# 16-column attention: where the softmax division is made

## The chip, the cores and the metric

The kernel runs on one core of one Trainium2 chip. The metric is the device time of one execution in microseconds. The kernel before was timed three times: 897.86, 899.01 and 900.95 us, median 899.01 us.

The core has five engines that matter here, each with its own in-order instruction stream, which meet through semaphores: TensorE (PE, with its weight loads PEld), VectorE (DVE), ScalarE (ACT), GpSimd (POOL) and SyncE (SP), which only issues DMAs. GpSimd does not touch the matmul accumulators (PSUM, 8 banks); TensorE writes them, VectorE and ScalarE read them.

## The reference

64 images of 96x96x3 are cut into 36 patches each (2304 tokens of 192 features). The tokens then go through: an embedding, a causal attention with 12 heads of 64 columns ("wide", the code calls the stage attn1), a layer with attention and an MLP, and a second layer with attention and a mixture of experts. The attentions of the last two layers are the ones that change. Each has 12 heads of 16 columns over the 36 tokens of one image:

```python
# attention of the MLP layer (stage attn2)
a = softmax(einsum('bhnd,bhmd->bhnm', q, k) * hd ** -0.5, axis=-1)     # hd = 16
o = einsum('bhnm,bhmd->bhnd', a, v).transpose(0, 2, 1, 3).reshape(B, N, C)
o = o @ w_proj + b_proj
# attention of the expert layer (stage attn3): the same with a bias -slope[h] * |n - m| on the scores
```

softmax is exp(s - max) divided by its sum over m. The division commutes with the product by v: it may be done to the probabilities, or to o.

## The kernel before, in words

Both attentions are made by one function, `narrow_stage` (L808). It works on units of two images (72 tokens, `UNIT`), 32 units in all, in groups of four units (288 tokens, `WIDE`), 8 groups. Every engine walks steps k = 0 .. 34 in program order; step k holds pieces of several units, so that the stage is a software pipeline. Within a step, in order:

- TensorE (`tensor`): `scores(k)`, six matmuls with q as weights and head-masked keys as data (L1032, L1036), into PSUM banks 2 and 3 or 4 and 5 in turn; `mix(k-3)`, eight matmuls of 108 rows by 36 columns, probabilities times values (L1064), into bank 6; the next group's work, by k mod 4: transposes of x (L983), projections of q and k (L994 to L998, two of three chunks, then one), values (L1013); `turn(k-2)`, four transposes of the probabilities (L1047), into bank 6 as well, so that it waits for `copy_z(k-3)`; then `project_out(t)` (L1073, L1074) for each tile of 128 tokens that is complete, 18 tiles in all.
- VectorE (`vector`): `take_scores(k)`: row maximum and subtraction (attn2: L1302, L1304), or bias addition and row maximum (attn3: L1295, L1300); `sum_up(k-1)`: row sums of the exponentials, 100x432 to 100x12 (L1311), and the reciprocal of these 12 columns (L1316); by k mod 4 the split of x (L1262, L1263), the masked keys (L1270, L1271) and in attn2 the layer norm in front (L1237 to L1253); `post_norm` in attn3 (L1335), and `add_residual(t)` (L1320, in attn3 also L1325 to L1329).
- ScalarE (`scalar`): `exponentiate(k-1)` (L1176), `copy_z(k-3)` from bank 6 into the ring z_t (L1193, L1195), the group's roundings and copies, `copy_turned(k-2)` (L1183).
- GpSimd (`gpsimd`): in attn3 `shift(k)`, subtraction of the maximum (L938); `normalise(k-1)`, the 100x432 probabilities times the broadcast reciprocal (L931); small powers (L920, L925), and the split of weights for the stage that follows (L2599 to L2619).
- SyncE (`sync`): once a group, after its last value block is copied, `spread_values` issues nine DMAs (L897) that place the values block by block; `mix` of the group's first unit waits for them. Weight loads for later stages follow in the same queue.

The values carry a column of ones (L951), which brings the bias row of the output projection in. While attn2 ends, the MLP begins (`tail`); attn3 is followed by the experts. `keep_going` (L337) issues matmuls without a use where TensorE would stand still.

## Time and profile before

| | us |
|---|---|
| median of three runs | 899.01 |
| profiled execution | 903.05 |
| its span | 901.3 |
| TensorE busy | 818.9 |
| VectorE busy | 542.0 |
| ScalarE busy | 439.9 |
| GpSimd busy | 408.7 |

The span is what the profile covers; 1.75 us of the profiled execution lie around it. attn2 takes the stretch from about 292 to 412 us, attn3 that from about 534 to 677 us. "Busy" counts each instruction from its start to its end. The ends of matmuls are modelled, so a busy TensorE can still have room.

### The profile page before, as it was taken

To read this page: it belongs to the slowest core of one execution; us is meant where nothing else is said; L and a number is where in the kernel's file an instruction comes from. 1 tells how busy PE (TensorE), PEld (TensorE's weight loads), DVE (VectorE), ACT (ScalarE), POOL (GpSimd) and SP (SyncE) were. 2 spreads that over 40 slices of the span, in tenths; PEclk is the share of its full clock that TensorE was granted. 3 is DMA by queue.
4 is the path that set the end of the run, shared out by engine and by line. 5 is a ranking of instruction groups with operands and counts; after the bars stand their busy time and mean duration, and the time that the engine had idled before them with its cause. 6 is when DMAs were issued, how large, how long until landed. Compare 5 with 4: busy or idle time off the path is not lost. (4 is left out here: it accounts for less than half of the span.)

```text
span 901.3 us, 21350 instructions
## 1 busy us (share of the span) xinstructions
PE 818.9 (91%) x7767; PEld 733.5 (81%) x7767; DVE 542.0 (60%) x1467; ACT 439.9 (49%) x1094; POOL 408.7 (45%) x489
## 2 busy tenths in 40 slices
PE   9899999999998898987999989888879999999973
PEld 8889998899997676766999976666657899899973
DVE  2235565556665898993763337788966622467645
ACT  0246555555644576763345527566626221355523
POOL 1534444344444544342442236767841455244444
PEclk9999999999999999996999989898979999999996
DMA  9910111111110232225200013623200111333252
GB/s 308 265 51 21 31 27 37 31 32 30 37 37 2 35 67 26 34 22 172 24 1 1 1 27 50 157 47 65 46 3 2 36 60 63 81 99 107 77 170 94
DMA packets 103942, 55.78 MB, mean 62 GB/s; under 512 B 67264, under 2 KB 94512, under 8 KB 103840
## 3 DMA queue, kind: packets, MB, share of 16 engines
q1 hardware_dynamic: 99248, 45.99, 21.2%
q0 software_dynamic: 3792, 7.84, 2.5%
q8 instruction: 64, 1.05, 0.5%
q10 hardware_dynamic: 800, 0.59, 0.2%
q14 instruction: 38, 0.31, 0.1%
HBM read 29.81 MB, written 13.97 MB: 49 GB/s over the span
## 5 line engine op out<-in xcount | busy, mean ns | idle before, releaser
L931 POOL TENSOR_TENSOR attn_prob<-attn_prob,attn_recip 100x432 f32<-100x432 f32 x64 | 58.6, 916 | 67.1 <-DVE attn_recip L1316 66.6
L450 POOL TENSOR_TENSOR attn_prob_x<-attn_prob,attn_recip 100x864 f32<-100x864 f32 x32 | 52.6, 1644 | 52.8 <-DVE attn_recip L759 52.8
L1892 POOL DMA_INDIRECT results<-moe_hid_shared x43 | 41.1, 955 | 58.1 <-ACT moe_hid_shared L2107 58.1
L1602 ACT ACTIVATE mlp_hid<-psum,columns 128x384 f32<-128x384 f32 x72 | 38.1, 580 | 41.4 <-PE psum L96 41.4
L1047 PE MATMUL psum<-ident,attn_prob 100*108 100x100 f32 x256 | 35.5, 264 | 21.4 <-POOL attn_prob L931 12.9
L1047 PEld LDWEIGHTS psum<-ident,attn_prob 100*108 100x108 f32 x256 | 26.1, 138 | 27.2 <-POOL attn_prob L931 18.7
L1064 PEld LDWEIGHTS psum<-attn_prob_t,attn_values 108*49 108x49 f32 (+1 forms) x1024 | 33.7, 132 | 15.5 <-ACT attn_prob_t L1183 6.7
L1176 ACT ACTIVATE attn_prob<-attn_prob 100x432 f32<-100x432 f32 x64 | 36.1, 564 | 19.0 <-POOL attn_prob L938 17.8
L2082 ACT ACTIVATE moe_silu<-psum 128x384 f32<-128x384 f32 x36 | 17.7, 491 | 56.5 <-PE psum L107 56.5
L1064 PE MATMUL psum<-attn_prob_t,attn_values 108*49 108x36 f32 (+1 forms) x1024 | 36.0, 217 | 8.3 <-DMA attn_values<-attn_v_tok 5.0
L1555 PE MATMUL psum<-mlp_w_dn_s,mlp_hid 128*128 128x192 f32 (+2 forms) x306 | 42.6, 290 | 0.0
L436 POOL TENSOR_TENSOR attn_rstd<-attn_var_eps,neg_half 128x1 f32<-128x1 f32 x18 | 10.2, 568 | 71.3 <-DVE attn_var_eps L771 71.3
L1970 PE MATMUL psum<-w_dn_shared,moe_hid_shared 128*128 128x192 f32 x216 | 38.7, 342 | 3.7 <-DVE moe_hid_shared L2257 3.7
L1555 PEld LDWEIGHTS psum<-mlp_w_dn_s,mlp_hid 128*128 128x128 f32 x306 | 42.0, 191 | 0.0
L1970 PEld LDWEIGHTS psum<-w_dn_shared,moe_hid_shared 128*128 128x128 f32 x216 | 37.8, 201 | 4.1 <-DVE moe_hid_shared L2257 4.0
L686 ACT ACTIVATE attn_z_t<-psum 128x432 f32<-128x432 f32 (+2 forms) x32 | 16.2, 507 | 50.6 <-PE psum L566 50.5
L938 POOL TENSOR_TENSOR attn_prob<-attn_prob,attn_row_max 100x432 f32<-100x432 f32 x32 | 29.1, 910 | 25.7 <-DVE attn_row_max L1300 25.7
L2496 PE MATMUL psum<-embed_w_tok,embed_patches 128*128 128x192 f32 x216 | 37.1, 329 | 3.9 <-DMA embed_patches<-in_x 3.1
L2496 PEld LDWEIGHTS psum<-embed_w_tok,embed_patches 128*128 128x128 f32 x216 | 34.8, 190 | 5.9 <-DMA embed_patches<-in_x 4.6
L576 PE MATMUL psum<-w_o,attn_z_t 128*128 128x192 f32 x216 | 38.7, 329 | 0.9 <-ACT attn_z_t L686 0.6
L1455 POOL TENSOR_TENSOR mlp_rstd<-mlp_var_eps,neg_half 128x1 f32<-128x1 f32 x18 | 10.6, 587 | 63.3 <-DVE mlp_var_eps L1671 63.3
L1311 DVE TENSOR_REDUCE attn_row_sum<-attn_prob 100x12 f32<-100x432 f32 x64 | 38.0, 594 | 2.0 <-ACT attn_prob L1176 1.7
(474 smaller groups left out, 2790.5 us busy)
## 6 DMA issues: line engine op xcount, KB each, us to landing
embed_patches<-in_x SPq DMA_DIRECT2D x8, 768.0 KB, 14.5
sorted_rows<-mlp_pad_zeros SPq DMA_DIRECT2D x1, 4214.0 KB, 15.6
moe_hid_shared<-sorted_rows SPq DMA_DIRECT2D x43, 98.0 KB, 2.1
attn_v<-attn_v_tok SPq DMA_DIRECT2D x16, 216.0 KB
attn_values<-attn_v_tok SPq DMA_DIRECT2D x96, 27.0 KB
side_raw_a<-in_w_gu_dram SPq DMA_DIRECT2D x8, 288.0 KB, 3.2
side_raw_b<-in_w_gu_dram SPq DMA_DIRECT2D x16, 144.0 KB, 3.4
h_rows<-results SPq DMA_DIRECT2D x6, 288.0 KB, 5.4
```

The lines of the kernel that those rows point to most:

```text
L450: nc.gpsimd.tensor_tensor(prob_x[k % 2][:, :, :, :], prob[k % 3][:, :, :].rearrange("p h (a n) -> p h a n", a=1) .to_broadcast([QP, HEADS, ...
L576: last = nc.tensor.matmul(out_ps, z_t[:, c, at:at + P], w_o[:, c, :], start=(c == 0), stop=(c == chunks - 1))
L931: nc.gpsimd.tensor_tensor(pr, pr, recip[k % 2][:, :].rearrange("p (h a) -> p h a", a=1) .to_broadcast([QP, HEADS, SEQ]), ALU.mult).then_in ...
L1047: last = nc.tensor.transpose(bank(6)[0:3 * SEQ, n * P:n * P + QP], flat[:, n * 3 * SEQ:(n + 1) * 3 * SEQ], ident[0:QP, 0:QP])
L1064: last = nc.tensor.matmul(ps[r:r + m, n // 2, a * SEQ:(a + 1) * SEQ], v[:, n, 0:m], prob_t[k % 2][:, n, a, :], start=True, stop=True)
L1176: nc.scalar.activation(prob[k % 3][:, :, :], prob[k % 3][:, :, :], ACT.Exp).then_inc(S["exp_done"], 1)
L1311: nc.vector.tensor_reduce(row_sum[:, :], prob[k % 3][:, :, :], axis=AX.X, op=ALU.add).then_inc(S["sum_ready"], 1)
L1555: last = nc.tensor.matmul(bank(3 + t)[:, 0:w.shape[1]], hid_step(n)[:, t * MT:(t + 1) * MT], w, start=(n == 0), stop=(n == 17), skip_group ...
L1602: nc.scalar.activation(hid_step(n), bank(n % 3)[:, 0:MW], ACT.Gelu, bias=b_up[:, c:c + 1]).then_inc(S["gelu_done"], 1)
L1892: nc.gpsimd.indirect_dma_start(out=results, out_offset=bass.IndirectOffsetOnAxis(ap=x_in[j % x_ring][:, D:D + 1].bitcast(U32), axis=0), in ...
L1970: last = nc.tensor.matmul(bank(4 + n % 2)[:, 0:D], hid_of(i)[:, c, t * P:(t + 1) * P], w_dn_shared[:, c, :], start=(c == 0), stop=(c == sh ...
L2496: last = nc.tensor.matmul(out_bank(t), patches[:, t, c, :], w_tok[:, c, :], start=(c == 0), stop=(c == chunks - 1))
```

## The change

Nothing is divided before the mixing any more. The exponentials go to `turn`, `copy_turned` and `mix` as they are, each a step (turn) or a step less a piece (mix) earlier than before. A new piece `add_up(k)` multiplies the turned probabilities by a constant block `head_ones` (108x64: ones where row and column belong to the same head of the three), which puts each head's sum, over 36 rows, into the 16 columns of that head, in the same layout as z: 128 x 2 x 72. The block is made once, by a memset and three affine_select of GpSimd, each waiting for the one before. VectorE inverts this whole block out of bank 5 (`invert_sums`), ScalarE copies z unchanged into `z_raw`, and GpSimd multiplies both into z_t (`divide_z`). `sum_up` and `normalise` are gone. The scores have one pair of banks instead of two, the probabilities two buffers instead of three, and the turned probabilities have bank 4 for themselves.

```diff
-    prob = [sb(f"prob{p}", [QP, HEADS, SEQ]) for p in range(3)]
+    prob = [sb(f"prob{p}", [QP, HEADS, SEQ]) for p in range(2)]
-    row_sum = sb("row_sum", [QP, HEADS])
-    recip = [sb(f"recip{p}", [QP, HEADS]) for p in range(2)]
+    head_ones = sb("head_ones", [3 * SEQ, 64])
+    recip = [sb(f"recip{p}", [P, 2, UNIT]) for p in range(2)]
+    z_raw = [sb(f"z_raw{p}", [P, 2, UNIT]) for p in range(2)]
...
+    scores_ps = psum[:, 2 * BANK:4 * BANK].rearrange("p (s n) -> p s n", s=4)[:, 0:3, 0:4 * SEQ].rearrange(
+        "p s (h n) -> p s h n", h=4)
+    turned_ps = bank(4).rearrange("p (g a n) -> p g a n", g=4, a=2)
     z_ps = bank(6)[:, 0:2 * UNIT].rearrange("p (c n) -> p c n", c=2)
+    sums_ps = bank(5)[:, 0:2 * UNIT].rearrange("p (c n) -> p c n", c=2)
...
 # gpsimd
-        def normalise(k):
+        def divide_z(k):
             pool.wait_ge(S["recip_ready"], k + 1)
+            pool.wait_ge(S["z_copied"], k + 1)
...
+            ins = nc.gpsimd.tensor_tensor(z_t[:, :, at:at + n], z_raw[k % 2][:, :, 0:n], recip[k % 2][:, :, 0:n],
+                                          ALU.mult)
+            if n < UNIT:
+                ins = nc.gpsimd.tensor_tensor(z_t[:, :, 0:UNIT - n], z_raw[k % 2][:, :, n:UNIT],
+                                              recip[k % 2][:, :, n:UNIT], ALU.mult)
+            ins.then_inc(S["z_divided"], 1)
...
         clear(0)
+        nc.gpsimd.memset(head_ones[:, :], 1.0).then_inc(S["ones_placed"], 1)
+        pool.wait_ge(S["ones_placed"], 1)
+        nc.gpsimd.affine_select(out=head_ones[:, 0:48], in_=head_ones[:, 0:48], compare_op=ALU.is_ge, fill=0.0, base=0,
+                                pattern=[[-SEQ, 3], [0, 16]], channel_multiplier=1).then_inc(S["ones_placed"], 1)
...
         clear(1)
...
+            if k >= 3:
+                divide_z(k - 3)
             if bias_hk is not None and k < units:
                 shift(k)
-            if 1 <= k <= units:
-                normalise(k - 1)
...
 # tensor, scores(k)
-            if k >= 2:
-                pe.wait_ge(S["scores_taken" if bias_hk is not None else "shifted"], k - 1)
+            if k >= 1:
+                pe.wait_ge(S["scores_taken" if bias_hk is not None else "shifted"], k)
 # turn(k)
-            pe.wait_ge(S["normalised"], k + 1)
+            pe.wait_ge(S["exp_done"], k + 1)
             if k >= 1:
                 pe.wait_ge(S["turned_copied"], k)
-                pe.wait_ge(S["z_copied"], k)
...
+        def add_up(k):
+            pe.wait_ge(S["turned_copied"], k + 1)
+            if k == 0:
+                pe.wait_ge(S["ones_placed"], 4)
+            else:
+                pe.wait_ge(S["recip_ready"], k)
+            for n in range(4):
+                r, m = 64 * (n % 2), 64 if k == 0 else 49
+                last = nc.tensor.matmul(sums_ps[r:r + m, n // 2, :], head_ones[:, 0:m],
+                                        prob_t[k % 2][:, n, :, :].rearrange("p a q -> p (a q)"), start=True, stop=True)
+            last.then_inc(S["added_up"], 1)
 # project_out(t)
-            pe.wait_ge(S["z_copied"], -(-P * (t + 1) // UNIT))
+            pe.wait_ge(S["z_divided"], -(-P * (t + 1) // UNIT))
 # order of a step
-            if k >= 3:
-                mix(k - 3)
...
             if 2 <= k < units + 2:
-                turn(k - 2)
+                add_up(k - 2)
+                mix(k - 2)
+            if 1 <= k <= units:
+                turn(k - 1)
...
 # scalar: copy_turned(k - 1) instead of (k - 2), at the same place; copy_z(k)
-            ins = nc.scalar.activation(z_t[:, :, at:at + n], z_ps[:, :, 0:n], ACT.Copy)
+            if k >= 2:
+                act.wait_ge(S["z_divided"], k - 1)
+            nc.scalar.activation(z_raw[k % 2][:, :, :], z_ps[:, :, :], ACT.Copy).then_inc(S["z_copied"], 1)
 # vector, take_scores(k)
-            if k >= 3:
-                dve.wait_ge(S["turned"], k - 2)
+            if k >= 2:
+                dve.wait_ge(S["turned"], k - 1)
...
-        def sum_up(k):
-            dve.wait_ge(S["exp_done"], k + 1)
-            dve.wait_ge(S["recip_ready"], k)
-            nc.vector.tensor_reduce(row_sum[:, :], prob[k % 3][:, :, :], axis=AX.X, op=ALU.add
-                                    ).then_inc(S["sum_ready"], 1)
-            dve.wait_ge(S["sum_ready"], k + 1)
+        def invert_sums(k):
+            dve.wait_ge(S["added_up"], k + 1)
             if k >= 2:
-                dve.wait_ge(S["normalised"], k - 1)
-            nc.vector.reciprocal(recip[k % 2][:, :], row_sum[:, :]).then_inc(S["recip_ready"], 1)
+                dve.wait_ge(S["z_divided"], k - 1)
+            nc.vector.reciprocal(recip[k % 2][:, :, :], sums_ps[:, :, :]).then_inc(S["recip_ready"], 1)
...
+            if k >= 3:
+                invert_sums(k - 3)
             if k < units:
                 take_scores(k)
-            if 1 <= k <= units:
-                sum_up(k - 1)
```

## Rows read from the trace of the kernel before

**Rows 1.** The page's busy times: engine, busy us, share of the span, instructions.
```profile
PE 818.9 (91%) x7767; PEld 733.5 (81%) x7767; DVE 542.0 (60%) x1467; ACT 439.9 (49%) x1094; POOL 408.7 (45%) x489
```

**Rows 2.** Busy time by stretch: steady parts of attn2 and attn3.
```profile
core 0: us, PE busy (x) PEld busy (x) DVE busy (x) ACT busy (x) POOL busy (x), PEclk, DMA share, GB/s
309.00:396.00 87.00, 79.91 (x1067) 64.19 (x1068) 78.18 (x174) 64.24 (x177) 37.06 (x54) 0.98 0.24 37
552.00:650.00 98.00, 85.84 (x1093) 67.86 (x1094) 83.45 (x189) 62.88 (x161) 73.66 (x84) 0.93 0.39 79
```

**Rows 3.** Groups of VectorE by shape: xcount, busy us, mean ns, idle before.
```profile
L1311 DVE TENSOR_REDUCE attn_row_sum<-attn_prob 100x12 f32<-100x432 f32 x64 | 38.0, 594 | 2.0 <-ACT attn_prob L1176 1.7
L1302 DVE TENSOR_REDUCE attn_row_max<-psum 100x12 f32<-100x432 f32 x32 | 19.1, 596 | 2.0 <-PE psum L1036 1.6
L1316 DVE RECIPROCAL attn_recip<-attn_row_sum 100x12 f32<-100x12 f32 x64 | 14.6, 228 | 2.2
L1325 DVE BATCH_NORM_STATS2 attn_stats<-h_rows 128x6 f32<-128x192 f32 x18 | 6.5, 361 | 0.6
L1320 DVE TENSOR_TENSOR x_tok<-psum,h_rows 128x192 f32<-128x192 f32 x18 | 6.2, 347 | 16.4 <-PE psum L1074 16.2
```

**Rows 4.** The same view, small and 144-column operations of VectorE.
```profile
L1329 DVE TENSOR_SCALAR attn_var_eps<-attn_mean_var 128x1 f32<-128x1 f32 x18 | 2.8, 154 | 0.6
L2199 DVE TENSOR_TENSOR moe_earlier<-psum,moe_iota 128x144 f32<-128x144 f32 x1 | 0.3, 308 | 0.2 <-PE psum L1948 0.2
L2752 DVE TENSOR_SCALAR columns<-columns 64x1 f32<-64x1 f32 x1 | 0.1, 132 | 0.0
```

**Rows 5.** Timeline (start us, us) of TensorE in attn2: mix, half a projection, turn.
```profile
313.05 0.53 PE L1064 MATMUL psum<-attn_prob_t,attn_values 108*49 108x36 f32 x16
...
315.08 0.52 PE L1073 MATMUL psum<-w_o,attn_z_t 128*128 128x192 f32 x2
...
318.79 0.51 PE L1047 MATMUL psum<-ident,attn_prob 100*108 100x100 f32 x4
```

**Rows 6.** Waits, 300 to 412 us (attn2): us in total, times, longest.
```profile
POOL attn_prob L931 <- DVE attn_recip L1316: 63.6, 28, 6.1
PE psum L1047 <- POOL attn_prob L931: 3.7, 5, 1.4
PE psum L1047 <- ACT attn_z_t L1193: 3.7, 3, 2.3
```

**Rows 7.** Waits, 545 to 672 us (attn3).
```profile
PE psum L1047 <- POOL attn_prob L931: 9.2, 6, 3.2
DVE h_rows L1320 <- PE psum L1074: 10.0, 4, 5.6
PE psum L1047 <- ACT attn_z_t L1193: 3.4, 8, 0.9
```

**Rows 8.** Groups of GpSimd by shape.
```profile
L931 POOL TENSOR_TENSOR attn_prob<-attn_prob,attn_recip 100x432 f32<-100x432 f32 x64 | 58.6, 916 | 67.1 <-DVE attn_recip L1316 66.6
L461 POOL TENSOR_TENSOR h_rows<-h_rows,vectors 128x192 f32<-128x192 f32 x18 | 10.3, 596 | 10.1 <-DVE vectors L2775 10.1
L2604 POOL TENSOR_TENSOR w_router_a_lo<-side_raw_a,w_router_a_hi 128x10 fp32r<-128x10 f32 x1 | 0.2, 208 | 0.0
```

**Rows 9.** One line of VectorE, L1335: duration min, median, max.
```profile
L1335 DVE TENSOR_SCALAR h_rows<-h_rows,attn_mean_var,attn_rstd x18: 379/419/3193, 560.6 to 676.8; 128x192 f32<-128x192 f32 x18
```

**Rows 10.** Timeline around the values' DMAs and the first mixes in attn3.
```profile
542.34 7.51 SPq L897 DMA_DIRECT2D attn_values<-attn_v_tok  x9
551.16 0.66 PE L1064 MATMUL psum<-attn_prob_t,attn_values 108*64 108x36 f32 x16 [1.49 <-DMA attn_values<-attn_v_tok]
...
581.18 0.89 PE L1064 MATMUL psum<-attn_prob_t,attn_values 108*49 108x36 f32 x16 [3.48 <-DMA attn_values<-attn_v_tok]
```

**Rows 11.** Timeline: one projection matmul in each attention's head.
```profile
293.09 0.29 PE L995 MATMUL psum<-ring_a_lo,w_qkv_a_hi 128*128 128x288 f32 x1
...
535.72 0.44 PE L995 MATMUL psum<-ring_a_lo,w_qkv_a_hi 128*128 128x288 f32 x1
```

More of the change, by code:

```diff
@@ L953, in gpsimd @@
         clear(0)
+        nc.gpsimd.memset(head_ones[:, :], 1.0).then_inc(S["ones_placed"], 1)
+        pool.wait_ge(S["ones_placed"], 1)
+        nc.gpsimd.affine_select(out=head_ones[:, 0:48], in_=head_ones[:, 0:48], compare_op=ALU.is_ge, fill=0.0, base=0,
+                                pattern=[[-SEQ, 3], [0, 16]], channel_multiplier=1).then_inc(S["ones_placed"], 1)
+        pool.wait_ge(S["ones_placed"], 2)
+        nc.gpsimd.affine_select(out=head_ones[:, 0:48], in_=head_ones[:, 0:48], compare_op=ALU.is_ge, fill=0.0,
+                                base=SEQ - 1, pattern=[[SEQ, 3], [0, 16]], channel_multiplier=-1
+                                ).then_inc(S["ones_placed"], 1)
+        pool.wait_ge(S["ones_placed"], 3)
+        nc.gpsimd.affine_select(out=head_ones[:, 48:64], in_=head_ones[:, 48:64], compare_op=ALU.is_ge, fill=0.0,
+                                base=SEQ - 1, pattern=[[0, 16]], channel_multiplier=-1
+                                ).then_inc(S["ones_placed"], 1)
         clear(1)
@@ L1040, in turn @@
         def turn(k):
[L1041 removed]
+            pe.wait_ge(S["exp_done"], k + 1)
             if k >= 1:
                 pe.wait_ge(S["turned_copied"], k)
[L1044 to L1045 removed]
+            flat = prob[k % 2][:, :, :].rearrange("p h n -> p (h n)")
             for n in range(4):
[L1047 removed]
+                last = nc.tensor.transpose(bank(4)[0:3 * SEQ, n * P:n * P + QP],
                                            flat[:, n * 3 * SEQ:(n + 1) * 3 * SEQ], ident[0:QP, 0:QP])
@@ L1221, in scalar @@
                 side.round_step(act, g - 1)
-            if 2 <= k < units + 2:
-                copy_turned(k - 2)
+            if 1 <= k <= units:
+                copy_turned(k - 1)
             if g < groups and j == 1:
```

33 lines of the change are left out of this document (10 added, 23 removed).

## The prediction

> **What bounds the kernel now.** I read the busy times first: TensorE is busy 91% of the span, VectorE 60% [rows 1]. That is an average over stages. By stretch the two attentions look otherwise: in attn2's steady part TensorE has 79.91 of 87 us and VectorE 78.18, in attn3's 85.84 and 83.45 of 98 [rows 2]. So two engines are within 2% of each other, and ends of matmuls are modelled while VectorE's are not. Which of them sets the pace I take from who waits. In attn2 GpSimd waits 63.6 us for the reciprocal, that is for VectorE to come to it, while VectorE sat idle only 2.0 us before all its row maxima and 2.0 us before all its row sums [rows 3, 6]: VectorE works through its queue with 8.8 of 87 us idle, and the reader should see in it the engine to which time must not be added. TensorE's own waits are for what comes through the long chain exponential, sum, reciprocal, product, turn: 3.7 us for GpSimd and 3.7 us for the copy of z in attn2, 9.2 and 3.4 us in attn3 [rows 6, 7]. In attn3 VectorE waits 10.0 us for the output projection, 5.6 us of it at once [rows 7], behind a mix that stood 3.48 us for the values' DMAs [rows 10]. The other stages are not touched.
>
> **VectorE, the term that decides.** Removed per unit: the row sum, 594 ns, and the reciprocal of 12 columns, 228 ns [rows 3], 0.82 us. Added: one reciprocal of 144 columns. No row shows it at that size. From the rows: an operation has a part that does not grow. VectorE rows of one column take 132 and 154 ns, one of 144 columns 308 [rows 4], so the rate of ordinary operations is (308 - 154) / 143 = 1.08 ns a column. The reciprocal of 12 columns takes 228. With 132 ns fixed, 96 ns are left for 12 columns, 8.0 ns each, and 144 columns take 132 + 144 x 8.0 = 1.28 us. With 154 ns fixed it is 6.2 ns each and 1.04 us. From below: if the excess were a fixed cost of the operation, 132 further columns at the ordinary rate give 228 + 143 = 0.37 us [rows 4]. From above: with nothing fixed, 228 x 12 = 2.74 us. I take 1.28: a fixed part must exist, the one-column rows measure it, and 228 ns lies far off the 166 ns (154 + 11 x 1.08) that a 12-column operation of ordinary rate would take. The change is then 1.28 - 0.82 = +0.46 us a unit, 32 x 0.46 = +14.7 us in each attention if VectorE sets the pace throughout.
>
> **TensorE.** Added per unit: four matmuls of 108x49 weights on 72 columns. A mix is eight of 36 columns with the same weights' size, the same 288 columns in all, and takes 0.53 us [rows 5]; so I take 0.5 us, and bound it by half of that and by 0.6. Over 64 units 32 to 34 us. Removed is no matmul, only waits before the turn, for GpSimd and for the copy of z: 7.4 us in attn2 and 12.6 us in attn3 [rows 6, 7]. Against VectorE: in the steady part of attn2 (87 us, 25 units of 3.5 us) VectorE needs 78.2 + 25 x 0.46 = 89.7 us of work and TensorE 79.9 + 12.5 = 92.4, of which the modelled ends are a part; with the 8.8 us that VectorE now loses between instructions and in short waits, 98.5 us. VectorE stays the later one, and the addition on TensorE is hidden behind it. If it is not hidden it is the first rival below.
>
> **GpSimd.** 916 ns a unit go (L931). A product of 128x144 lies between 10 columns, 208 ns, and 192, 596 ns [rows 8]: 208 + 134 x 2.13 = 0.49 us; two of 16 units wrap in the ring and pay a second start. GpSimd gets 64 x 0.42 = 27 us back, off the path. But L1335 on VectorE, 0.379 us at its shortest, stretches to 3.193 us when GpSimd runs beside it, 18 of them with a median of 0.419 [rows 9]; with GpSimd less busy I give back 2 us in attn3 (bounds 0 and 5).
>
> **Order and buffers.** `invert_sums(k-3)` stands first in VectorE's step. `add_up(k-2)` waits for it, and behind it on TensorE stand mix, turn and the output projection. `add_residual`, the last piece of VectorE's step, waits for that projection. So in a step with a complete tile (18 of 32) the loop is: reciprocal 1.28, add_up 0.5, mix 0.53, turn 0.51, projection 0.8 (two of 0.4), residual 0.35 [rows 3, 5], some 4.0 us; in attn3 its statistics follow, 0.36 and two operations under 0.2 with a wait each, 4.8 us. VectorE's own work in a step without group work is 1.28 + 1.2 (two like the 0.596 of L1302) + 0.35 = 2.8 us, in attn3 4.1 with the statistics and L1335. The gap of about 1 us counts only where k mod 4 brings no group work, five or so steps in a stage, and a part of it is in today's waits: +3 us in each (bounds 0 and 6). One pair of banks for the scores: scores(k) waits for take_scores(k-1), which VectorE does right after its reciprocal, before TensorE is through with step k-1; nothing. Two buffers of probabilities: take_scores(k) waits for turn(k-2), a step earlier on TensorE; nothing. In attn3 VectorE has 14.6 us of idle in 98 [rows 2]; the chain through sum, reciprocal and product no longer stands in front of the turn, so a part of that idle is work time now: -5 us (bounds 0 and -10).
>
> **The values' DMAs.** Nine issues take 7.51 us, and the first mix ran 8.8 us after the first of them, after a wait of 1.49 us [rows 10]. The mix of a group's first unit now stands at the end of the third step instead of the start of the fourth, in front of a turn and of the next scores. In steady state that leaves the rest of a step and two and a half more, of at least 3.5 us each, some 11 us, more than 8.8. At the head of each stage the wait is there, and scores(3) and a turn now stand behind it: +1 us each, +2. The stall of 3.48 us stays. Building head_ones, four short GpSimd instructions of some 0.2 us, as the one of 10 columns [rows 8], delays only the clearing of the second group's buffers and one small power behind it: +0.3.
>
> **Sum.** 14.7 + 14.7 (VectorE) + 6 (loop) - 5 (idle taken) - 2 (L1335) + 2 + 0.3 (heads of stages) = +30.7 us on the profiled execution's 903.05 us (span 901.3 and 1.75 around it): 933.8. The median of the runs is 4.0 us below the profiled one, so 929.7; I say 929.
>
> **The rivals.**
> - *TensorE sets the pace.* For: 92.4 us of work against 89.7 as computed above. Against: modelled ends, and VectorE's waits for it are short. Then the cost is 34 us less the 20 us of waits, +14: 913.
> - *The reciprocal is cheap, and the change pays.* The place is VectorE's queue; it decides from a 144-column reciprocal under the 0.82 us removed. At 0.37 us VectorE gives back 29 us. TensorE's 34 us then have to lie in its idle time, 7.1 of 87 and 12.2 of 98 us, which over both stages (scaled to 32 units each: 9 and 15 us) is 24, and in what a full clock would give back, 7% of some 120 us and 2% of another, 11 us: -1 at that, and -5 with L1335 as well: 894. Against it stands the 228 ns row.
> - *TensorE's clock.* It was granted 0.98 in attn2 and 0.93 in attn3 [rows 2]. A TensorE that waits for VectorE at each step stands still more often, and at the lower level (1.2 GHz) a projection matmul takes 0.44 us instead of 0.29 [rows 11], 0.15 more. A group has 15 of these and as many of the values, some 4 us in all with its other matmuls. If a third of its work fell there, +0.7 us in 16 groups, +11: 940.
> - *Nothing changes* because both engines had room: would need the loss of 0.46 us a unit to fall into VectorE's 9% idle, 8.8 us in 25 units against 11.5 added. It cannot be whole.
>
> **Chances.** Forecast 0.70, TensorE 0.12, clock 0.10, cheap reciprocal 0.06, nothing 0.02. The time is 929. A reciprocal of 1.04 us would take off 64 x 0.24 = 15 us (914), and the first rival lies at 913; no idle taken, no gain at L1335 and the loop at its upper bound add 13 (942). Range 910 to 944. A difference of 0.3% (2.7 us) is about what this kernel's measurement can tell. Faster 0.07, same 0.03, slower 0.90.
>
> **What would show it.** Right: a 144-column reciprocal of 1.2 to 1.35 us, x64; VectorE busy above 90% in both attentions; the group period 2 us longer in attn2, a little less in attn3; TensorE's waits now at add_up, for the reciprocal; GpSimd's product near 0.5 us; no wait for GpSimd before a turn. Wrong: a reciprocal under 0.8 us; VectorE idle rising while TensorE has none; granted clock under 0.9 in attn2.

## The result, and the profile after

| us | before | after |
|---|---|---|
| median, runs side by side | 899.96 (897.86 to 900.95) | 930.06 (927.59 to 934.26) |
| profiled execution | 903.05 | 927.59 |
| its span | 901.3 | 925.9 |

The ratio is 1.034, 95% interval 1.030 to 1.039. 929 was forecast, 910 to 944. The total came out; the reasons did so only in part.

First the busy times on the page, answering to [rows 1].

```profile
PE 846.4 (91%) x8279; PEld 745.8 (81%) x8279; DVE 548.8 (59%) x1403; ACT 436.1 (47%) x1086; POOL 385.7 (42%) x505
```

Then the two stretches of [rows 2].

```profile
309.00:396.00 87.00, 81.93 (x1165) 61.33 (x1162) 74.04 (x138) 55.99 (x158) 24.07 (x50) 1.00 0.23 36
552.00:650.00 98.00, 87.83 (x1118) 65.03 (x1117) 75.75 (x135) 57.25 (x140) 56.12 (x79) 0.93 0.37 75
```

The kernel is 25 us longer by its span, and VectorE's total busy time grew by 7. In both stretches its share fell: 78.18 to 74.04 of 87 us, 83.45 to 75.75 of 98. The second stretch exaggerates this, because attn3 begins 12.6 us later in the kernel after; over each kernel's own seven group periods (defined below) the share fell from 89% to 83% in attn2 and from 84% to 80% in attn3. An engine that sets the pace doesn't get idler when it is given more work.

The new operations on the page: xcount, busy us, mean ns of one, and what ended the idle time before.

```profile
L1340 DVE RECIPROCAL attn_recip<-psum 128x144 f32<-128x144 f32 x64 | 67.4, 1054 | 6.0 <-PE psum L1097 5.7
L938 POOL TENSOR_TENSOR attn_z_t<-attn_z_raw,attn_recip 128x144 f32<-128x144 f32 (+1 forms) x64 | 30.2, 472 | 114.6 <-DVE attn_recip L1340 78.2
L1097 PE MATMUL psum<-attn_prob_t,attn_head_ones 108*49 108x72 f32 (+1 forms) x512 | 31.1, 244 | 16.3 <-DVE attn_recip L1340 15.5
```

The reciprocal takes 1.054 us, not 1.28. The product takes 0.49 us whole (472 ns with the wrapped ones). TensorE has a new wait, 15.5 us for the reciprocal, in front of `add_up`.

Where the time is: SyncE's timeline (start us, duration) has the values' DMAs once a group, so that eight starts give seven periods of each stage. Before, the first and last of attn2 and the last of attn3 (attn3's first is the 542.34 of [rows 10]):

```profile
298.30 7.52 SPq L897 DMA_DIRECT2D attn_values<-attn_v_tok  x9
...
395.93 7.85 SPq L897 DMA_DIRECT2D attn_values<-attn_v_tok  x9
...
646.69 7.49 SPq L897 DMA_DIRECT2D attn_values<-attn_v_tok  x9
```

After, the first and last of both:

```profile
297.80 7.52 SPq L899 DMA_DIRECT2D attn_values<-attn_v_tok  x9
...
404.35 7.85 SPq L899 DMA_DIRECT2D attn_values<-attn_v_tok  x9
...
554.93 7.51 SPq L899 DMA_DIRECT2D attn_values<-attn_v_tok  x9
...
668.97 7.49 SPq L899 DMA_DIRECT2D attn_values<-attn_v_tok  x9
```

A group's period went from 97.63 / 7 = 13.95 us to 106.55 / 7 = 15.22 in attn2, and from 14.91 to 16.29 in attn3. By stretch, the 24.6 us of the span are: -0.5 up to attn2's first group, +8.9 over its seven periods, +4.2 from there to attn3's first (attn2's last group and attn3's start), +9.7 over attn3's periods, +2.3 behind them. All later runs are read by these two periods.

Who waits, 555 to 705 us of the kernel after, answering to [rows 7]:

```profile
DVE h_rows L1344 <- PE psum L1107: 19.3, 17, 3.6
PE psum L1097 <- DVE attn_recip L1340: 11.7, 10, 3.5
```

VectorE waits for the output projection, 19.3 us where it was 10.0 [rows 7] (12.2 over the whole of attn3 before), and TensorE waits for VectorE's reciprocal. Two engines that wait for each other are the sign of a loop. One step and the next, on both engines' timeline (weight loads, the scores, the projections, the values and other work left out):

```profile
627.25 0.36 DVE L1344 TENSOR_TENSOR h_rows<-psum,h_rows 128x192 f32<-128x192 f32 x1 [1.32 <-PE psum L1107]
...
629.60 0.46 PE L1097 MATMUL psum<-attn_prob_t,attn_head_ones 108*49 108x72 f32 x8 [0.78 <-DVE attn_recip L1340]
...
630.59 1.42 DVE L1299 SCALAR_TENSOR_TENSOR attn_keys_b<-psum,columns,head_mask 64x1152 f32<-64x1152 f32 x1
...
631.09 0.49 PE L1107 MATMUL psum<-w_o,attn_z_t 128*128 128x192 f32 x2
...
632.04 1.51 DVE L1359 TENSOR_SCALAR h_rows<-h_rows,attn_mean_var,attn_rstd 128x192 f32<-128x192 f32 x1
...
633.59 0.36 DVE L1344 TENSOR_TENSOR h_rows<-psum,h_rows 128x192 f32<-128x192 f32 x1
...
633.98 0.36 DVE L1349 BATCH_NORM_STATS2 attn_stats<-h_rows 128x6 f32<-128x192 f32 x1
...
634.74 1.06 DVE L1340 RECIPROCAL attn_recip<-psum 128x144 f32<-128x144 f32 x1
635.72 0.55 DVE L1323 TENSOR_TENSOR attn_prob<-psum,bias 100x432 f32<-100x432 f32 x1
...
635.95 0.61 PE L1097 MATMUL psum<-attn_prob_t,attn_head_ones 108*49 108x72 f32 x8 [1.78 <-DVE attn_recip L1340]
```

In the first of the two steps each engine waits for the other: VectorE 1.32 us for the projection, then TensorE 0.78 us for the reciprocal that stands behind the residual. In the second, VectorE waits for nothing: the projection of 631.09 was long done when VectorE came to its residual at 633.59. The sums that the second reciprocal inverts lay in the bank since about 630; it came at 634.74 because it is queued behind the masked keys, the post-norm, the residual and its statistics of the step before. TensorE stood 1.78 us for it, and its next `add_up` took 0.61 us instead of 0.46.

### The profile page after: what moved, and what is told of

It reads as the page before. It is cut to its first block and busy times, and to the rows that moved or that the text cites. A ratio compares the mean times of both kernels' runs of the same rounds, so it can differ in the third digit from the quotient of the medians.

```text
span 925.9 us, 22390 instructions
## 1 busy us (share of the span) xinstructions
PE 846.4 (91%) x8279; PEld 745.8 (81%) x8279; DVE 548.8 (59%) x1403; ACT 436.1 (47%) x1086; POOL 385.7 (42%) x505
## 5 line engine op out<-in xcount | busy, mean ns | idle before, releaser
L938 POOL TENSOR_TENSOR attn_z_t<-attn_z_raw,attn_recip 128x144 f32<-128x144 f32 (+1 forms) x64 | 30.2, 472 | 114.6 <-DVE attn_recip L1340 78.2
L1340 DVE RECIPROCAL attn_recip<-psum 128x144 f32<-128x144 f32 x64 | 67.4, 1054 | 6.0 <-PE psum L1097 5.7
L1217 ACT ACTIVATE attn_prob_t<-psum 108x288 f32<-108x288 f32 x64 | 26.2, 409 | 77.7 <-PE psum L1068 77.7
L1097 PE MATMUL psum<-attn_prob_t,attn_head_ones 108*49 108x72 f32 (+1 forms) x512 | 31.1, 244 | 16.3 <-DVE attn_recip L1340 15.5
L1097 PEld LDWEIGHTS psum<-attn_prob_t,attn_head_ones 108*49 108x49 f32 (+1 forms) x512 | 21.5, 131 | 29.2 <-issue 26.3
L1085 PE MATMUL psum<-attn_prob_t,attn_values 108*49 108x36 f32 (+1 forms) x1024 | 36.7, 217 | 6.1 <-ACT attn_z_raw L1224 4.0
L553 PE MATMUL psum<-ident,attn_prob_x 100*72 100x100 f32 x384 | 38.4, 249 | 0.0
L2281 DVE TENSOR_TENSOR moe_hid_shared<-psum,moe_silu 128x384 f32<-128x384 f32 x36 | 20.0, 556 | 30.8 <-PE psum L107 30.6
```

The costliest lines, as they stand in the source:

```text
L553: last = nc.tensor.transpose(bank(3 + p)[0:UNIT, n * P:n * P + QP], prob_x[k % 2][:, 4 * p + n, :, :].rearrange("p a n -> p (a n)"), ident ...
L938: ins = nc.gpsimd.tensor_tensor(z_t[:, :, at:at + n], z_raw[k % 2][:, :, 0:n], recip[k % 2][:, :, 0:n], ALU.mult)
L1085: last = nc.tensor.matmul(ps[r:r + m, n // 2, a * SEQ:(a + 1) * SEQ], v[:, n, 0:m], prob_t[k % 2][:, n, a, :], start=True, stop=True)
L1097: last = nc.tensor.matmul(sums_ps[r:r + m, n // 2, :], head_ones[:, 0:m], prob_t[k % 2][:, n, :, :].rearrange("p a q -> p (a q)"), start=T ...
L1340: nc.vector.reciprocal(recip[k % 2][:, :, :], sums_ps[:, :, :]).then_inc(S["recip_ready"], 1)
```

## The experiments

All were timed side by side with the kernel before, and the medians of before lie between 897.0 and 899.4 in these groups. "Period" is a group's, attn2 / attn3; before it is 13.95 / 14.91, after 15.22 / 16.29.

| kernel | us | ratio to before, 95% | period |
|---|---|---|---|
| after | 930.06 | 1.030 to 1.039 | 15.22 / 16.29 |
| after, copy in place of reciprocal | 914.61 | 1.012 to 1.022 | 15.07 / 15.13 |
| after, add_up twice | 933.31 | 1.033 to 1.047 | 15.83 / 17.01 |
| after, one sum matmul of four | 927.10 | 1.027 to 1.037 | 15.19 / 16.20 |
| after, two banks for sums | 939.97 | 1.042 to 1.052 | 16.04 / 17.18 |
| after, reciprocal ahead of residual | 911.48 | 1.008 to 1.017 | 15.37 / 15.89 |
| the same, mix early | 959.32 | 1.067 to 1.072 | 19.90 / 18.16 |
| after, mix early only | 998.24 | 1.110 to 1.116 | 20.96 / 21.33 |
| mix early, reciprocal behind scores | 913.50 | 1.012 to 1.020 | 15.53 / 15.93 |
| mix early and a step later | 945.79 | 1.049 to 1.055 | 16.81 / 16.54 |
| before, a second reciprocal | 901.61 | 0.999 to 1.007 | 13.83 / 14.86 |
| before, sum matmuls added | 901.45 | 0.999 to 1.006 | 14.10 / 14.26 |
| before, the new banks | 899.48 | 0.994 to 1.003 | 14.25 / 14.51 |

### Is it VectorE's or TensorE's busy time?

**A copy in place of the reciprocal.** The inversion is left out.

```diff
-            nc.vector.reciprocal(recip[k % 2][:, :, :], sums_ps[:, :, :]).then_inc(S["recip_ready"], 1)
+            nc.vector.tensor_copy(recip[k % 2][:, :, :], sums_ps[:, :, :]).then_inc(S["recip_ready"], 1)
```

> The changed kernel with VectorE's 144-column reciprocal replaced by a copy of the same block (the inversion is left out, so z is multiplied by the sums). VectorE's 144-column rows take 0.31 us, the reciprocal 1.06, so 0.75 us a unit leave VectorE, 48 us over 64 units. If VectorE's queue, with the loop that runs through it (V), sets the pace: far below the changed kernel's 930, down to where TensorE takes over, 890 to 900, that is at or below the kernel before (900). If the four matmuls added on TensorE are the cost (T): little changes, 920 or more.

914.61 us, between the two expectations. The copy takes 304 ns, so 64 x 0.75 = 48 us of VectorE's work went for 15.5 us of time. By the profiled spans (17.4 us) 8.1 us lie over attn3's seven periods, 3.9 between the stages' groups, 3.8 behind attn3's last group and 1.0 over attn2's, and TensorE's wait for this line fell from 15.5 to 6.7 us. With VectorE at 59.79 of 87 us busy attn2's period is 15.07 still. So in attn2 VectorE's busy time has next to nothing to do with the loss, and even a cheap operation at this place leaves the kernel 1.7% slower than before.

**More work for VectorE in the kernel before:** the small reciprocal issued twice, the first into a spare buffer.

```diff
+            nc.vector.reciprocal(spare[:, :], row_sum[:, :])
             nc.vector.reciprocal(recip[k % 2][:, :], row_sum[:, :]).then_inc(S["recip_ready"], 1)
```

> The kernel before with one more reciprocal of 12 columns a unit on VectorE (0.228 us, into a tile that nobody reads), about what the change adds to VectorE per unit (1.058 - 0.822 = 0.236 us). In all 14.6 us. V: +11 to +15, 911 to 915. If VectorE has room and only the new order costs (L or T): under +4.

```profile
L1317 DVE RECIPROCAL attn_spare<-attn_row_sum 100x12 f32<-100x12 f32 x64 | 14.6, 228 | 2.2
L1318 DVE RECIPROCAL attn_recip<-attn_row_sum 100x12 f32<-100x12 f32 x64 | 10.9, 170 | 0.0
```

The second one takes 170 ns right behind the first: 10.9 us of added work. The net addition of the change is 1.054 - 0.822 = 0.232 us a unit, 14.8 us. The 10.9 us cost 2.5 us by the ratio 1.003, whose interval goes from nothing to 5.8 us. VectorE's queue was the place, but not the pace.

**More work for TensorE in the kernel before:** the four matmuls of `add_up`, with a constant as weights, into a spare part of bank 6.

```diff
+                    if a == 1:
+                        last = nc.tensor.matmul(bank(6)[r:r + 49, UNIT * (2 + n // 2):UNIT * (3 + n // 2)],
+                                                ident[0:3 * SEQ, 0:49],
+                                                prob_t[k % 2][:, n, :, :].rearrange("p a q -> p (a q)"),
+                                                start=True, stop=True)
```

> The kernel before with the four added matmuls alone (108x49 weights, 72 columns, a unit), behind the mix, into columns of bank 6 that nobody reads. New theory after the first four runs (P): in the kernel before, TensorE and not VectorE sets the pace of attn2, since 0.23 us more a unit on VectorE there moved the group period from 13.95 to 13.83 us, that is not at all; the four matmuls, 0.28 us a unit, 1.1 a group, are what attn2 lost. P expects a period of 15.0 to 15.2 us in attn2 (15.22 in the changed kernel) and 910 to 918 in all, since nothing of TensorE's waits is removed here. Old theory (V): under +5, 904 at most.

Its stretches, as in [rows 2]:

```profile
309.00:396.00 87.00, 82.84 (x1251) 66.95 (x1250) 75.74 (x172) 62.33 (x173) 37.03 (x54) 1.00 0.24 37
552.00:650.00 98.00, 90.96 (x1354) 72.76 (x1356) 88.28 (x199) 66.23 (x168) 77.20 (x88) 1.00 0.41 80
```

901.45 us, no difference that can be told. The period grew by 0.15 us in attn2 and fell by 0.65 in attn3, where the granted clock was 1.00 in place of 0.93. The two traces overstate this: the one here is of the fastest of ten executions (895.42 us, clock 0.981 over the whole run), that of before is of a slow one (903.05 us, 0.961). Over all executions of the group the mean clock is 0.972 with the added matmuls (ten) and 0.967 before (nineteen). At a clock of 0.968 to 0.973 eight executions with them take 902.1 us on average and six of before 896.8. So the added matmuls cost some 5 us at an equal clock, and a slightly higher clock hides about half of it. The work itself is not what costs 30 us.

**Doubling and quartering it in the kernel after.** `for n in (0, 1, 2, 3, 0, 1, 2, 3)` in one, `range(4 if k == 0 else 1)` in the other (the sums of nine heads stay those of unit 0).

> The changed kernel with each of the four matmuls of add_up issued twice. In the trace add_up starts 0.26 to 0.29 us before the mix that follows it, so 0.28 us a unit more on TensorE, 18 us over 64 units. T: +18, 948. V: only the steps in which VectorE waits for the output projection feel it (18 of 32 in a stage, 36 in all, less those with slack): +4 to +10, 934 to 940.

> The changed kernel with one of the four matmuls of add_up from the second unit on (the sums of nine heads are left as the first unit's). 0.2 us a unit leave TensorE. P: attn2's period falls from 15.22 by up to 0.8 us, attn3's by about as much as e2's doubling raised it (0.7), in all -8 to -12, 918 to 922. V: -2, 928.

933.31 and 927.10 us, with 930.06 between: by the ratios its doubling costs 5 us and three quarters of it taken away give back 2, and the intervals of all three overlap. `add_up`'s busy time rose from 31 to 47 us in the first. Its periods grew by 0.61 and 0.72 us a group, more than half of the added 1.1, so in the kernel after more TensorE work is not hidden; the second's fell by 0.03 and 0.09 only.

### Is it the place of the reciprocal?

**Two banks for the sums.** z and sums of a unit share bank 5 or 6 in turn, so that `add_up(k)` need not wait for the reciprocal of unit k-1; ScalarE's copy of z now waits for the reciprocal of its own unit.

```diff
 # add_up
-                pe.wait_ge(S["recip_ready"], k)
+            if k >= 2:
+                pe.wait_ge(S["z_copied"], k - 1)
 # copy_z
-            act.wait_ge(S["mixed"], k + 1)
+            act.wait_ge(S["recip_ready"], k + 1)
 # invert_sums
-            dve.wait_ge(S["added_up"], k + 1)
+            dve.wait_ge(S["mixed"], k + 1)
```

> The changed kernel with sums and z of a unit together in bank 5 or 6 in turn, so that add_up(k-2) no longer waits for the reciprocal of unit k-3; the copy of z waits for the reciprocal instead, because two engines may not read one bank at once. The work of each engine is the same. If the loop reciprocal, add_up, mix, turn, projection, residual, reciprocal costs time beyond VectorE's own work (L): 8 to 15 us less, 915 to 922. If VectorE's busy time alone counts: within 2 us of 930.

```profile
ACT attn_z_raw L1226 <- DVE attn_recip L1342: 36.7, 20, 3.7
```

939.97 us, a miss. TensorE's wait went, but the row (waits, 555 to 705 us) shows what I put in its place: ScalarE stands 36.7 us for the late reciprocal, and everything queued behind `copy_z` with it. The run moved the wait and so tells nothing of the bank.

**The reciprocal ahead of the residual.** In VectorE's step k it now inverts unit k-2 ahead of `add_residual`, instead of unit k-3 at the start of the next step.

```diff
-            if k >= 3:
-                invert_sums(k - 3)
             if k < units:
                 take_scores(k)
...
             for t in ready_tiles(k - 1):
                 post_norm(t)
+            if 2 <= k < units + 2:
+                invert_sums(k - 2)
             for t in ready_tiles(k):
                 add_residual(t)
```

> The changed kernel with the reciprocal moved: unit k-2 is inverted at the end of VectorE's step k, ahead of the residual, instead of at the start of step k+1 behind it. VectorE waits 19 us in attn3 and 11 us in attn2 for the output projection, and in attn3 the reciprocal behind it is what add_up waits for (11.7 us). L (in attn3 the loop projection, residual and statistics, reciprocal, add_up is the cost): attn3's period from 16.29 to about 15.3, close to the 15.13 of the copy; attn2 changed by less than 0.3; 920 to 924 in all. If VectorE's busy time is the cost: no change, 929 to 931.

The group of the reciprocal, and the wait of 555 to 705 us, as of the kernel after:

```profile
L1340 DVE RECIPROCAL attn_recip<-psum 128x144 f32<-128x144 f32 x64 | 67.4, 1054 | 16.1 <-PE psum L1097 15.2
```

```profile
DVE h_rows L1344 <- PE psum L1107: 7.1, 7, 4.0
```

911.48 us, 18.6 less (by the ratios 1.034 and 1.013 some 19), with the same work on every engine. The reciprocal now waits for its sums, 15.2 us against 5.7, and not they for it: TensorE waits 5.1 us for it over the run instead of 15.5, VectorE 7.1 us for the projection instead of 19.3. That is the largest amount that any run takes back, shown by moving one line of the program.

It is not all the loop. I had expected 920 to 924, all by attn3's period falling by 1.0 us; it fell by 0.40. Of the 12.5 us by which the profiled span is shorter (the trace is of the slowest of four executions here, and of the fastest of four after), 2.8 lie over attn3's periods, 3.1 between the stages' groups and 7.8 behind attn3's last values' DMAs; attn2 got 1.2 longer. The 7.8 are more than the 2.3 that the change had lost there. 6.8 of them lie in the stretch from those DMAs to attn3's last statistics (L1349). It is, in the kernel after and here:

```profile
668.97:699.70 30.73, 22.81 (x267) 16.56 (x263) 18.67 (x41) 8.26 (x22) 15.04 (x21) 0.83 0.08 8
664.30:688.20 23.90, 18.62 (x266) 13.49 (x262) 18.81 (x40) 8.34 (x22) 14.93 (x22) 1.00 0.10 11
```

The same matmuls take 22.81 us at a granted clock of 0.83 and 18.62 at 1.00, so 4.2 of the 6.8 us go with the clock (the kernel before has 28.61 us at 0.76). The two runs further down that also invert unit k-2 in step k have this short end too, 22.8 and 23.2 us at 1.00; all that invert unit k-3 have 26.5 to 32.0 us at 0.74 to 0.94.

**The new banks in the kernel before.** One pair for the scores, the turned probabilities in bank 4 and no wait of `turn` for the copy of z.

```diff
-                pe.wait_ge(S["scores_taken" if bias_hk is not None else "shifted"], k - 1)
+                pe.wait_ge(S["scores_taken" if bias_hk is not None else "shifted"], k)
```

> The kernel before with the change's PSUM layout alone: one pair of banks for the scores, the turned probabilities in bank 4, so that turn no longer waits for the copy of z. The division stays where it was. The waits for that copy were 3.7 us in attn2 and 3.4 us in attn3, at places that set the pace by P: 893 to 898. If the one pair of score banks costs: 900 or more.

899.48 us: the banks cost nothing that can be told, in sum (attn2 +0.30 a group, attn3 -0.40, one trace each).

### What is left: the order on TensorE

With the reciprocal moved 12 us stay. Before, `mix` stood right behind the scores; after, it stands behind the group's work. The rows show a price of that at the seams, where one block of matmuls follows another (TensorE's timeline in attn2, before):

```profile
326.04 0.44 PE L1036 MATMUL psum<-attn_keys_b,attn_q_b 128*36 128x144 f32 x4
326.31 0.53 PE L1064 MATMUL psum<-attn_prob_t,attn_values 108*49 108x36 f32 x16
```

and after:

```profile
319.81 0.29 PE L1020 MATMUL psum<-ring_b,w_qkv_b_lo 128*128 128x288 f32 x1
320.03 0.46 PE L1097 MATMUL psum<-attn_prob_t,attn_head_ones 108*49 108x72 f32 x8
...
329.23 0.44 PE L1058 MATMUL psum<-attn_keys_b,attn_q_b 128*36 128x144 f32 x4
329.60 0.33 PE L1005 MATMUL psum<-ident,attn_x_hat 128*128 128x128 f32 x1
...
332.47 0.44 PE L1058 MATMUL psum<-attn_keys_b,attn_q_b 128*36 128x144 f32 x4
333.01 0.19 PEld L1016 LDWEIGHTS psum<-ring_a_hi,w_qkv_a_hi 128*128 128x128 f32 x1 [0.39 <-DVE ring_b L1291]
333.01 0.40 PE L1016 MATMUL psum<-ring_a_hi,w_qkv_a_hi 128*128 128x288 f32 x1
```

From the start of the last scores to that of the next block it is 0.27 us in the median of 25 before. After it is 0.37 to 0.38 in 16 of 24 cases (300 to 395 us), whether transposes, projections or values follow. In the other eight TensorE waited for data: so in the last pair above, whose 0.54 us hold a wait of the weight load for VectorE's split of x. The end of the group's work has a like price: from the last projection to the turn 0.13 us before, to `add_up` 0.22 to 0.23 after; and from the turn to the next scores 0.44 before, 0.48 after. From the mix on nothing changed (0.46). That is 0.10 + 0.10 + 0.04, some 0.24 us a unit or 1.0 a group, an estimate of 15 us in 64 units where TensorE's queue sets the pace. The third of the runs below, which has the old order again with all of the new work, has the old prices again in the same stretch (only behind its mix it pays 0.03 more):

```profile
321.56 0.44 PE L1058 MATMUL psum<-attn_keys_b,attn_q_b 128*36 128x144 f32 x4
321.83 0.42 PE L1097 MATMUL psum<-attn_prob_t,attn_head_ones 108*49 108x72 f32 x8
...
325.00 0.29 PE L1020 MATMUL psum<-ring_b,w_qkv_b_lo 128*128 128x288 f32 x1
325.13 0.51 PE L1068 MATMUL psum<-ident,attn_prob 100*108 100x100 f32 x4
```

On this the Trainium skill has a rule, "TensorEngine Tiling (Array Packing)", section "Key Properties": a change of the tiling mode drains the engine. The rows agree in so far as the dearer seams (0.37 and 0.23 us) lie between a block whose weights have 36 or 49 columns and one with 108 or 128, and the cheaper ones (0.27 and 0.13 us) between two blocks of like width; but no run here tells a drain from the wait for new weights.

Three runs put `add_up` and `mix` back behind the scores.

```diff
             if k < units:
                 scores(k)
...
+            if 2 <= k < units + 2:
+                add_up(k - 2)
+                mix(k - 2)
...
-            if 2 <= k < units + 2:
-                add_up(k - 2)
-                mix(k - 2)
             if 1 <= k <= units:
                 turn(k - 1)
```

ScalarE's `copy_z` goes ahead of `exponentiate` with it. The first has the earlier reciprocal too, the second only the move.

> The kernel with the reciprocal ahead of the residual addition, and now add_up and mix of unit k-2 on TensorE directly behind the scores of unit k, ahead of the group's projections, and ScalarE's copy of z ahead of its exponential. Theory 'the order on TensorE is the remaining loss' (the kernel before ran scores and mix as one unbroken run of matmuls; the changed one breaks the run twice more in a unit, some 0.1 us each, and its mix stands behind the group's work): about 12 us below the 911 of the kernel with the earlier reciprocal, 895 to 903, with a group's period in the first changed stage at 14.3 us or less against 15.37. Rival 'the order costs nothing, the rest is the clock and the group's own waits': 908 to 914, period unchanged. Third, 'mix now waits behind the scores for the copy of z or for the previous reciprocal': above 914, with TensorE's idle time ended by VectorE's reciprocal or ScalarE's copy.

> The changed kernel with only the move on TensorE and ScalarE (add_up and mix right behind the scores, copy of z ahead of the exponential), the reciprocal left at the start of VectorE's next step, behind the residual addition and the statistics. Theory 'the reciprocal's place and the order on TensorE are separate losses that add': about 12 us below 930, 915 to 921. Rival 'the early add_up now stands before a reciprocal that comes late, so the move is lost': 927 to 940, with TensorE's idle time in the scores-to-add_up gap ended by the reciprocal and well above the 11.7 us that it had in the second changed stage.

959.32 and 998.24 us, both far off: the first as its third theory has it, the second in the way of its rival but beyond the 940 that I gave it. TensorE and VectorE of the first (timelines):

```profile
339.20 0.44 PE L1058 MATMUL psum<-attn_keys_b,attn_q_b 128*36 128x144 f32 x4
341.79 0.46 PE L1097 MATMUL psum<-attn_prob_t,attn_head_ones 108*49 108x72 f32 x8 [2.15 <-DVE attn_recip L1340]
```

```profile
339.70 0.42 DVE L1290 TENSOR_TENSOR ring_a_lo<-attn_aff_a,ring_a_hi 128x256 fp32r<-128x256 f32 x1 [1.73 <-ACT ring_b L1166]
340.14 0.42 DVE L1291 TENSOR_TENSOR ring_b<-attn_aff_b,ring_b 64x256 fp32r<-64x256 f32 x1
340.59 1.06 DVE L1340 RECIPROCAL attn_recip<-psum 128x144 f32<-128x144 f32 x1
```

`add_up(k-2)` needs the reciprocal of unit k-3, and that one is queued behind the group's split of x, which waits for ScalarE, which waits for TensorE's transposes. Asking for it a piece earlier on TensorE made all of this part of the loop: 49.3 us of waits for the reciprocal over the run, 72.8 in the second. So the third run puts the reciprocal of unit k-2 right behind `take_scores(k)`, ahead of the group's work:

```diff
-            if k >= 3:
-                invert_sums(k - 3)
             if k < units:
                 take_scores(k)
+            if 2 <= k < units + 2:
+                invert_sums(k - 2)
             if j == 0 and g + 1 < groups:
                 split_x(g + 1)
```

> The kernel with add_up and mix of unit k-2 directly behind the scores of unit k, and VectorE's reciprocal of unit k-2 directly behind its taking of the scores of unit k, ahead of the split of x, the mask of the keys and the pre-norm. Theory 'in the last two runs add_up waited for the previous unit's reciprocal, which stood behind VectorE's work for the group': with the reciprocal ahead of that work the wait is gone, the loop is that of the kernel before, and what stays is 0.28 us of TensorE and 0.23 us of VectorE in a unit: 893 to 905 us, a group's period of 13.9 to 14.5 us in the first changed stage (before 13.95), TensorE's idle time before add_up under 5 us in 300 to 430 us. Rival 'the early mix itself is the loss (it waits for the copy of the turned probabilities or of z, whatever the reciprocal does)': 930 to 960, with that idle time still above 20 us but ended by ScalarE. Rival 'the reciprocal ahead of the split of x delays the group's chain by its 1.05 us, once in a group in each of 16 groups': 905 to 917.

Its waits, 300 to 410 us:

```profile
PE psum L1085 <- DMA attn_values<-attn_v_tok: 4.9, 5, 1.6
PE psum L1097 <- ACT attn_prob_t L1217: 4.0, 6, 1.5
```

913.5 us: the wait for the reciprocal is gone (26.0 to 0.2 us in 300 to 430 us) and 46 us with it, which settles the two misses. But it is no better than the 911.5. The time lies in the range of the last rival, a delayed split of x, but TensorE's waits for that split fell (2.0 us after, 0.3 here, 300 to 405 us), so that rival is not the reason. The mix of unit k-2 in this early place meets its values' DMAs and the copy of the turned probabilities, for which the kernel before had one step more. A last run takes units k-3 for `add_up`, `mix` and the reciprocal, at the same places, and leaves ScalarE as in the kernel after.

> The changed kernel with add_up and mix of unit k-3 (not k-2) directly behind the scores of unit k, where the kernel before had its mix, and the reciprocal of unit k-3 directly behind VectorE's taking of the scores of unit k; ScalarE's order is as in the changed kernel. Theory 'two losses stand against each other: TensorE's broken run of matmuls (mix behind the group's work) and the step of slack lost between the turn and the mix (mix of k-2 early waits for the copy of the turned probabilities and for the values' DMAs)': here both are mended, so a group's period in the first changed stage is 14.1 to 14.7 us (15.5 in the last run, before 13.95), TensorE's idle time before add_up and mix is under 3 us in 300 to 410 us, and the time is 897 to 907. Rival 'the output projection at the end of the step now waits for this unit's own product on GpSimd, which is 0.28, 1.2, 1.05 and 0.49 us behind the scores': 908 to 918, with TensorE's idle time before the output projection above 5 us in that window. Rival 'neither order nor slack, the period of 15.3 to 15.5 stays whatever is moved': 908 to 915 with no wait above 3 us.

Waits, 300 to 430 us:

```profile
PE psum L1106 <- POOL attn_z_t L938: 11.5, 11, 1.9
PE psum L1106 <- POOL attn_z_t L941: 6.4, 4, 2.4
```

945.79 us. The waits for DMAs and copies went, and the output projection at the end of the same step now stands for the product on GpSimd, 39 us over the run: the named rival, larger than I gave it.

What TensorE's time in attn2 goes to, from one start to the next of its blocks (waits included), us a group over seven groups:

| | scores, last part | add_up and mix | turn | x, projections, values | all |
|---|---|---|---|---|---|
| before | 1.51 | 2.00 | 1.55 | 5.28 | 13.95 |
| before, sum matmuls added | 1.69 | 2.76 | 1.46 | 4.60 | 14.10 |
| after | 2.05 | 2.83 | 1.61 | 5.08 | 15.22 |
| mix early, reciprocal behind scores | 1.89 | 3.89 | 1.55 | 4.60 | 15.53 |

(The columns leave out the other scores, the projection of z and what the trace has no record of. A wait is booked to the block ahead of it: the 5.28 of before hold those of the turn for GpSimd and of the transposes for x.) The second and third rows have the same matmuls in the old and in the new order. They differ by 0.36 us behind the last scores, 0.48 in the group's work and 0.15 behind the turn, 0.99 in all of the 1.12 between their periods, and the seams add up to 1.0. So most of what attn2 loses to the new order lies in these seams. Two limits: each row is one execution, the second at a granted clock of 1.00 over these groups and the third at 0.98; and no run has got these 15 us back, since each one that undid the order brought another wait. In the early order of the last row the group's work is at 4.60 again, but `add_up` and `mix` take 1.06 us more, for the waits shown above.

## Why the prediction was right or wrong

- **VectorE, "the term that decides": mis-sized and not the mechanism.** The reciprocal was taken at 1.28 us and measured 1.054, at the lower of the two sizes that I had from rows (1.04); the term is +0.23 us a unit, 14.8 us and not 29.4. "VectorE busy above 90%" came out as 85% and 77%, and the second reciprocal in the kernel before cost 2.5 us for 10.9 of work. What I took for the sign of a pace, GpSimd's 63.6 us for the reciprocal [rows 6], shows only that GpSimd had nothing else to do. The comparison "VectorE stays the later one" also gave VectorE its 8.8 us of idle time and TensorE nothing: 98.5 against 92.4. With TensorE's own 7.1 it is 99.5 on TensorE's side.
- **The loop, "+3 us in each": the step that was far too small.** I named it piece by piece (reciprocal, add_up, mix, turn, projection, residual, statistics) and then set it against VectorE's own work in a step, as though only the difference of 1 us counted, in five steps of a stage. Moving the reciprocal out of it gave 18.6 us. What I left out stands on the timeline above: VectorE's group work and post-norm lie in the same queue ahead of the residual and the reciprocal, so a turn can carry them too. How much of the 18.6 us is the loop itself stays open: of the 12.5 us by the spans 2.8 lie in attn3's steady part, where the prediction had placed it, none in attn2's, and the largest part in attn3's last group, where the clock rose with it.
- **TensorE hidden: nearly right, but not for the reason given.** Four matmuls on 72 columns took 0.28 us from their start to that of the mix, not 0.5 (the rows below). Their addition to the kernel before costs nothing that can be told, some 5 us at an equal clock; but it is not VectorE that hides it, and in the kernel after further matmuls lengthen the periods. The rival "TensorE paces" (913) fell with the same run.
- **Order on TensorE: left out.** I treated the move of `mix` behind the group's work as a matter of waits alone. The seams price it at some 0.24 us a unit, and most of attn2's loss lies there; it is the best account of the 12 us that stay, though no run has removed it alone.
- **Banks and buffers, "nothing": right**, by the run with the new banks. **GpSimd 0.49: right.** No wait for GpSimd before a turn: right.
- **"-5, idle taken": wrong in sign.** VectorE's idle time in the attn3 stretch rose from 14.6 to 22.3 us.
- **L1335, "-2":** now L1359, its longest 1.517 us (before 3.193 [rows 9]), its sum 8.8 us against 14.3. That is 5.5 us of VectorE's time, a little over my upper bound; the timeline of the loop shows one of the long ones still in it.
- **The clock:** 1.00 and 0.93, against 0.98 and 0.93. The rival of 940 did not occur. Its sum had a slip, since a third of 4 us a group is 1.3 and not 0.7; and in the rival of the cheap reciprocal -1 with 2 us for L1335 is -3, not -5.

So 930 against 929 is a sum of wrong terms. 29.4 us went to VectorE's busy time, for which the run with the second reciprocal speaks for 3.4 (2.5 / 10.9 x 14.8; 8 at the end of its interval); 6 went to the reciprocal's place in the loop, for which the moved reciprocal speaks for 18.6; and the 12 us that stay had no term. That the sum came within 1 us is luck.

## What to carry to other kernels

When a result that another engine needs is moved to the end of an in-order queue, price everything that is queued ahead of it, not its own duration: here moving a 1.05 us operation was worth 18.6 us, about as much as cutting it to 0.30 us in its place (15.5). An engine at 90% busy need not be the pace; add a small dummy operation to it, or look for two engines that wait for each other. Compare the starts of neighbouring blocks of matmuls before and after a reordering, and leave out the cases with a wait: a tenth of a microsecond at each of two seams and 0.04 at a third were 1 us a group here. In a software pipeline an order is a balance: of six rearrangements of the changed kernel two gained, 17 and 19 us, and four lost 10 to 68 us, each to one wait that the move brought into every group; none beat the kernel before.

## What the runs showed of the hardware

- A reciprocal costs 6.3 ns a column of float32 (128x144 out of a PSUM bank 1054 ns, 100x12 out of SBUF 228 ns; 170 ns right behind another one). A copy of the same 128x144 takes 304 ns.
- Four matmuls of 72 columns (108x49 weights) take 0.28 us from start to start, eight of 36 columns with the same weights' size 0.46: at these widths the number of matmuls costs more than the columns. TensorE's timeline after, in attn2 (add_up, mix, turn; the rows count x8 for the four that the code issues):

```profile
330.19 0.46 PE L1097 MATMUL psum<-attn_prob_t,attn_head_ones 108*49 108x72 f32 x8
330.47 0.52 PE L1085 MATMUL psum<-attn_prob_t,attn_values 108*49 108x36 f32 x16
330.93 0.55 PE L1068 MATMUL psum<-ident,attn_prob 100*108 100x100 f32 x4
```

- From the start of one block of matmuls to the next: 0.27 us from the last scores to a mix (108x49 weights), 0.37 to a projection (128x128); 0.13 us from the last projection to a turn (100x108), 0.23 to `add_up` (108x49).
- The granted clock moved with small changes of the program: in attn3's last group it was 0.83 in the kernel after (30.73 us, TensorE busy 22.81) and 1.00 with the reciprocal moved (23.90 us, 18.62). With 256 matmuls added to the two attentions of the kernel before the mean clock of ten executions was 0.972 instead of 0.967.
